# Edge stage of a graph attention layer: running sums kept in two accumulator banks, queries in two rounded parts, a product in four instructions

## What is computed

```python
qkv = (h @ W_qkv + b_qkv).reshape(n, 3, H, DH)        # H = 8 heads of DH = 32
q, k, v = (qkv[:, 0], qkv[:, 1], qkv[:, 2])
score = jnp.einsum('ehd,ehd->eh', q[dst], k[src]) * SCALE
mx = jax.ops.segment_max(score, dst, num_segments=n)
ex = jnp.exp(score - mx[dst])
denom = jax.ops.segment_sum(ex, dst, num_segments=n)
attn = ex / denom[dst]
msg = attn[:, :, None] * v[src]
h_new = jax.ops.segment_sum(msg, dst, num_segments=n)
h_out = jnp.transpose(h_new, (0, 2, 1)).reshape(n, DIM)
return (h_out + h) @ W_out + b_out
```

## Time and profile before

| what | value |
|---|---|
| three runs, us | 2121.98, 2125.84, 2130.7 (median 2125.84) |
| span of the profiled execution, us | 2134.3 |
| mean granted clock of TensorE | 0.903 |
| busy over the whole span | PE 83%, DVE 72%, POOL 54%, ACT 50% |
| gathers of the edge stage (L1740) | 440, busy 476.1 us, mean 1082 ns, idle before them 135.8 us |
| queries (L1822) | 880 matmul records, busy 233.7 us, mean 407 ns |
| sums (L1853) | 880 matmul records, busy 226.2 us, mean 402 ns |
| message product (L1896) | 110, mean 1219 ns |

### The profile page before, as it was taken

One profiled execution on the slowest core, in us unless ns is written; L12 is line 12 of the kernel. 1 busy time (PEld: TensorE's weight loads), 2 busy tenths in 40 slices (PEclk: granted clock), 3 DMA queues, 4 the chain that ended last, 5 costly groups with the idle time before them and its releaser, 6 DMA issues. The chain is left out here.

```text
span 2134.3 us, 41549 instructions
## 1 busy us (share of the span) xinstructions
PE 1761.5 (83%) x10388; PEld 1537.1 (72%) x10389; DVE 1539.6 (72%) x2788; ACT 1070.3 (50%) x2353; POOL 1160.5 (54%) x1169
## 2 busy tenths in 40 slices
PE   3699999999999989828973868888888888866278
PEld 3499999999999979728972756666666766645267
DVE  5388888888888845643545849899999898847622
ACT  1677777777777726403420145445455454316133
POOL 0376666666666601462443457777777777512112
PEclk7799999999999989758996989999999999867579
DMA  3443333333333312133323566666666666524310
GB/s 96 133 121 111 104 108 108 104 107 108 105 106 108 98 31 80 69 124 98 119 75 98 193 185 189 189 188 188 193 191 186 190 187 188 148 65 141 115 38 29
DMA packets 132538, 267.55 MB, mean 125 GB/s; under 512 B 24030, under 2 KB 75888, under 8 KB 132407
## 3 DMA queue, kind: packets, MB, share of 16 engines
q0 software_dynamic: 63456, 191.61, 30.7%
q1 hardware_dynamic: 68534, 73.21, 11.2%
q10 hardware_dynamic: 416, 1.18, 0.2%
HBM read 225.34 MB, written 42.50 MB: 125 GB/s over the span
## 5 line engine op out<-in xcount | busy, mean ns | idle before, releaser
L319 POOL DMA_INDIRECT e_rows<-h_table,e_idx x440 | 453.4, 1030 | 214.1 <-issue 106.3
L1740 POOL DMA_INDIRECT a_rows<-kv_table,a_idx x440 | 476.1, 1082 | 135.8 <-issue 128.9
L619 PE MATMUL e_w<-w2h,e_hidl 128*128 128x256 f32 x880 | 247.7, 304 | 2.9 <-DVE e_msg L704 2.9
L589 PE MATMUL e_agg<-e_msg,e_hot 128*128 128x256 f32 x880 | 246.1, 402 | 0.0
L1822 PE MATMUL a_q<-q,a_spread 128*128 x880 | 233.7, 407 | 6.5 <-ACT a_spread L1782 6.3
L620 PE MATMUL e_w<-w2l,e_hidh 128*128 128x256 f32 x880 | 226.4, 280 | 0.0
L1853 PE MATMUL a_agg<-a_rows,x 128*128 128x264 f32 x880 | 226.2, 402 | 0.0
L704 DVE TENSOR_TENSOR e_msg<-e_w,e_rows 128x1024 f32<-128x1024 f32 x110 | 134.7, 1224 | 93.4 <-PE e_w L623 93.4
L1775 ACT ACTIVATE a_apart<-iota_n,dst_rel 128x128 f32<-128x128 f32 x440 | 140.6, 391 | 112.9 <-PE a_agg L1853 112.8
L1822 PEld LDWEIGHTS a_q<-q,a_spread 128*128 128x128 f32 x880 | 166.2, 199 | 38.9 <-issue 12.8
L1853 PEld LDWEIGHTS a_agg<-a_rows,x 128*128 128x128 f32 x880 | 168.2, 200 | 24.7
(11 more groups left out here) (456 smaller groups left out, 4221.4 us busy)
## 6 DMA issues: line engine op xcount, KB each, us to landing
e_ea<-in_eaT SPq DMA_DIRECT2D x220, 64.0 KB
m_rows<-expert_rows SPq DMA_DIRECT2D x32, 272.0 KB, 2.7
e_rows<-h_table,e_idx POOLq DMA_INDIRECT x440
a_rows<-kv_table,a_idx POOLq DMA_INDIRECT x440, 3.7
q_ab<-expert_out SPq DMA_DIRECT2D x50, 128.0 KB, 3.3
kv_table<-q_kv SPq DMA_DIRECT2D x25, 256.0 KB, 2.2
u_stage<-in_m_w SPq DMA_DIRECT2D x16, 256.0 KB
x<-in_x SPq DMA_DIRECT2D x1, 3200.0 KB, 13.9
```

The source lines that it names most:

```text
L319: c.nc.gpsimd.indirect_dma_start(out=rows[:, g.slot8, j, :], out_offset=None, in_=table, in_offset=bass.IndirectOffsetOnAxis(ap=idx[:, g.s ...
L589: last = mm(bank(wins[j]), hot[:, g.slot4, t, :], msg[:, g.slot4, t, :], start=False, stop=False, skip_group_check=True)
L619: mm(w, hidl[:, g.slot, cols[k]], w2h[:, k, :], start=(k == 0), stop=False)
L1740: nc.gpsimd.indirect_dma_start(out=rows[:, g.slot * IG + j, 0:2 * D], out_offset=None, in_=c.kv_dram, in_offset=bass.IndirectOffsetOnAxis( ...
```

## The change

Attention stage, window sums: they stay in PSUM. There are two banks, chosen by the window's parity; PE adds each item to the bank of its window (`add_item`), ACT copies the bank to `c.sums` after every item (`keep`), and the other bank is cleared by the two-column first instruction of each `add_item`. The sums run one step later (SUM = 7). DVE's addition is gone; its rescale works on the PSUM bank, at place 3 instead of 2, from a copy of the factors that ACT makes (`grown`). The first item's sum goes between the second and third query, or behind the queries at place 3; the second stays behind the transposes. `hot` has 12 slots. `c.sums` and the query parts now share one space, shifted by a window: a copied-out sum lies where a query was that is no longer needed.

Queries: `c.q` in float32 becomes `c.qhl`, a rounded float32r part and the rounded rest; each tile's query is two float32r matmuls. ACT makes the first part in `project_qkv`, POOL the second, ten windows behind.

Message product: four instructions of one tile instead of one of four.

POOL's clearing of `c.sums` is gone; the PSUM banks are zeroed by four ACT copies at the start of the stage.

```diff
@@ -1418,10 +1418,12 @@
+        q = c.sb("q_q", [P, GT, D], F32, s)
+        s_qh, s_ql = c.sem("q_qhigh"), c.sem("q_qlow")
...
@@ -1453,13 +1455,24 @@
+                BEHIND = 10
+                def query_low(t):
+                    need(pool, s_pg, (s_qh, t + 1))
+                    high, low = c.qhl[:, t, 0:D], c.qhl[:, t, D:2 * D]
+                    nc.gpsimd.tensor_tensor(low, q[:, t % GT, :], high.bitcast(F32), ALU.subtract).then_inc(s_ql, 1)
                 for t in range(NW):
                     need(pool, s_pg, (s_ab[t % RING], (t // RING + 1) * 16 * TOPK))
                     nc.gpsimd.tensor_tensor(ab[:, t % RING, 0, :], ab[:, t % RING, 0, :], ab[:, t % RING, 1, :], ALU.add).then_inc(s_pr, 1)
                     need(pool, s_pg, (s_pr, t + 1))
                     nc.gpsimd.tensor_tensor(window(c.x, t), window(c.x, t), ab[:, t % RING, 0, :], ALU.add).then_inc(s_x, 1)
-                nc.gpsimd.memset(c.sums[:, :, :], 0.0).then_inc(s_clr, 1)
-                pool.wait_ge(s_clr, 1)
+                    if t >= BEHIND:
+                        query_low(t - BEHIND)
+                for t in range(NW - BEHIND, NW):
+                    query_low(t)
+                pool.wait_ge(s_ql, NW)
...
@@ -1490,6 +1503,12 @@
+                def query_high(t):
+                    need(act, s_ag, (s_s, t + 1))
+                    nc.scalar.copy(c.qhl[:, t, 0:D], q[:, t % GT, :]).then_inc(s_qh, 1)
...
@@ -1501,6 +1520,10 @@
                         need(act, s_ag, (s_t, t + 1), (s_r, t - GT + 1))
                         nc.scalar.copy(xTh[:, t % GT, :, :], by_chunk(tp[t % 2])).then_inc(s_hi, 1)
+                    t = r - 1
+                    if inside(t):
+                        query_high(t)
+                query_high(NW - 1)
             @block.vector
             def _(dve):
@@ -1529,8 +1552,8 @@
-                        need(dve, s_dg, (s_ld, 32), (s_r, t + 1), (s_kv[t % GT], (t // GT) * 16))
-                        v.tensor_tensor(window(c.q, t), qp[t % 2][:, 0:D], b[:, 0:D], ALU.add)
+                        need(dve, s_dg, (s_ld, 32), (s_r, t + 1), (s_kv[t % GT], (t // GT) * 16), (s_ql, t - GT + 1))
+                        v.tensor_tensor(q[:, t % GT, :], qp[t % 2][:, 0:D], b[:, 0:D], ALU.add)
...
@@ -1688,11 +1711,13 @@
     nc = c.nc
     R, DM, ROW, LAG = Edges.RING, D + H, 2 * D + H, 6
+    SUM = LAG + 1
+    HR = 12
...
-        spread = c.sb("a_spread", [P, 2, IG, P], F32, s)
+        spread = c.sb("a_spread", [P, 2, IG, P], F32R, s)
...
@@ -1705,11 +1730,14 @@
-        hot = c.x[:, :, :].rearrange("p t d -> p (t d)")[:, 0:R * IG * P].rearrange("p (s n) -> p s n", n=P)
+        hot = c.x[:, :, :].rearrange("p t d -> p (t d)")[:, 0:HR * IG * P].rearrange("p (s n) -> p s n", n=P)
...
-        ap = c.ps("a_agg", [P, JG, 512], F32, s)
-        none = c.sb("a_none", [P, DM], F32R, s)
-        s_none = c.sem("a_none")
+        ap = c.ps("a_agg", [P, 2, 512], F32, s)
+        zero = c.x[:, :, :].rearrange("p t d -> p (t d)")[:, HR * IG * P:NW * D]
+        none = c.sb("a_none", [P, P], F32R, s)
+        s_zero, s_none = c.sem("a_zeroed"), c.sem("a_none")
+        bank = lambda w: ap[:, bass.ds(w & 1, 1), 0:DM].rearrange("p a d -> p (a d)")
+        other = lambda w: ap[:, bass.ds((w + 1) & 1, 1), 0:DM].rearrange("p a d -> p (a d)")
...
@@ -1718,7 +1746,10 @@
+        grown = c.sb("a_grown", [P, H], F32, s)
+        s_gn = c.sem("a_grown")
         four = lambda g: slice(g.slot * IG, (g.slot + 1) * IG)
+        hots = lambda g, j: (g.n % HR) * IG + j
...
                 nc.gpsimd.memset(none[:, :].bitcast(F32), 0.0).then_inc(s_none, 1)
+                nc.gpsimd.memset(zero[:, :], 0.0).then_inc(s_zero, 1)
...
-                        need(pool, c.sem("poolgate"), (s_idx, g.n + 1), (s_agg, g.n - R + 1))
+                        need(pool, c.sem("poolgate"), (s_idx, g.n + 1), (s_agg, (g.n - R + 1) * JG))
...
@@ -1744,9 +1776,22 @@
+                act.wait_ge(s_zero, 1)
+                for p in range(2):
+                    nc.scalar.copy(ap[:, p, 0:D], zero[:, :])
+                    nc.scalar.copy(ap[:, p, D:DM], zero[:, 0:H]).then_inc(s_zero, 1)
+                def keep(a, j, wins):
+                    need(act, s_ag, (s_agg, a.n * JG + j + 1))
+                    nc.scalar.copy(window(c.sums, wins[j])[:, 0:DM], bank(wins[j])).then_inc(s_acc, 1)
                 def step(at):
                     i = at(0)
+                    a = at(-SUM)
+                    if real(a):
+                        wins = item_windows(act, c, a.n)
+                        keep(a, 0, wins)
...
@@ -1770,16 +1815,21 @@
-                        need(act, s_ag, (s_agg, g.n - R + 1), (s_hot, g.n))
+                        need(act, s_ag, (s_agg, (g.n - HR + 1) * JG), (s_hot, g.n))
...
-                        nc.scalar.activation(hot[:, four(g), :], apart[:, :, :], ACT.Relu, bias=1.0, scale=-1.0).then_inc(s_hot, 1)
+                        nc.scalar.activation(hot[:, hots(g, 0):hots(g, IG), :], apart[:, :, :], ACT.Relu, bias=1.0, scale=-1.0).then_inc(s_hot, 1)
...
+                    if i.place == 2 and closed(i.chunk - 1):
+                        need(act, s_ag, (s_gr, i.chunk), (s_rs, 2 * (i.chunk - 1)))
+                        nc.scalar.copy(grown[:, :], grow).then_inc(s_gn, 1)
+                    if real(a):
+                        keep(a, 1, wins)
...
@@ -1798,65 +1848,76 @@
+                def add_item(m, j, both):
+                    own = (both + j) >> 1
+                    need(pe, None, (s_msg, m.n + 1), (s_acc, m.n * JG + j), *([(s_rs, 2 * m.chunk + 2)] if m.place == 0 and j == 0 else []), own=True)
+                    mm(other(own)[:, 0:2], none[:, :], none[:, 0:2], start=True, stop=False, skip_group_check=True)
+                    for half in range(CT):
+                        t = j * CT + half
+                        last = mm(bank(own), hot[:, hots(m, t), :], rows[:, m.slot * IG + t, D:ROW], start=False, stop=False, skip_group_check=True)
+                    last.then_inc(s_agg, 1)
                 def step(at):
...
-                        need(pe, None, (s_sc, min(i.n, NIG) if isinstance(i.n, int) else i.n), (s_rs, 2 * ch), own=True)
+                        need(pe, None, (s_sc, min(i.n, NIG) if isinstance(i.n, int) else i.n), (s_gn, ch), own=True)
...
+                    m = at(-SUM)
+                    sums = ahead.take(i.step, "sums", m.n) if real(m) else None
+                    late = i.place == 3
                     g = at(1)
+                    if real(m) and not real(g):
+                        add_item(m, 0, sums)
                     if real(g):
                         both = ahead.take(i.step, "q", g.n)
                         wins = both >> 1, (both + 1) >> 1
                         need(pe, None, (s_sp, g.n + 1), (s_pr, g.n - 1), own=True)
                         for j in range(IG):
+                            if j == CT and real(m) and not late:
+                                add_item(m, 0, sums)
                             if j == CT and i.place == 2 and closed(ch):
...
-                            last = mm(qp[g.pair][:, j * D:(j + 1) * D], spread[:, g.pair, j, :], window(c.q, wins[j // CT]), start=True, stop=True)
+                            both_parts = window(c.qhl, wins[j // CT])
+                            mm(qp[g.pair][:, j * D:(j + 1) * D], spread[:, g.pair, j, :], both_parts[:, 0:D], start=True, stop=False)
+                            last = mm(qp[g.pair][:, j * D:(j + 1) * D], spread[:, g.pair, j, :], both_parts[:, D:2 * D], start=False, stop=True)
                         last.then_inc(s_q, 1)
+                        if real(m) and late:
+                            add_item(m, 0, sums)
...
-                    m = at(-LAG)
-                    if real(m):
-                        moved = ahead.take(i.step, "sums", m.n) & 1
...
-                    if real(at(1 - LAG)):
-                        ahead.fetch(i.then, "sums", at(1 - LAG).n)
+                    if real(at(1 - SUM)):
+                        ahead.fetch(i.then, "sums", at(1 - SUM).n)
                     h = at(2)
                     if real(h):
                         need(pe, None, (s_hot, h.n + 1), (s_sp, h.n), own=True)
                         for j in range(IG):
-                            last = tr(hT[:, j * P:(j + 1) * P], hot[:, h.slot * IG + j, :], c.ident[:, :])
+                            last = tr(hT[:, j * P:(j + 1) * P], hot[:, hots(h, j), :], c.ident[:, :])
                         last.then_inc(s_ht, 1)
                     if i.place == 2 and closed(ch):
                         need(pe, None, (s_fi, 2 * ch + 2), (s_ex, ch + 1), own=True)
                         mm(grow, first[:, :], diag[:, :], start=True, stop=True).then_inc(s_gr, 1)
                     if real(m):
-
-                        need(pe, None, (s_msg, m.n + 1), (s_acc, m.n), own=True)
```

(47 more changed lines are left out.)

5 lines of the change are left out of this document (2 added, 3 removed).

## The result

The changed kernel takes 2190.28 us (median, 2188.22 to 2195.08) against 2126.73 (2121.98 to 2130.70) for the kernel before: ratio 1.0302, 95% interval 1.0283 to 1.0321. It is slower by 63.5 us; 15.9 were forecast, with a range up to 2168.

A forecast was written before the change was run, and what follows sets the result against it. POOL's stream was taken to pace the edge stage, at 22.15 us a chunk. Chunks +6.8, drain +7.2, projection +1.0 and start +0.9 gave +15.9 us: 2150 on the profiled 2134.3, 2142 on the median 2125.84; range 2100 to 2168.

The forecast's parts named there:

- Place 2 to 3: Edge stage, the chunk's longer step, through copies, four products, reductions, rescale and item 0: 7.13 us.
- Item 0 and its start, 1.11 + 0.03: Term of the ACT-PE round: item 0's matmuls 1.11 us, its two-column start 0.03 more (estimate), together 1.14.
- Two queries, 0.48: Term of the ACT-PE round: two queries in two parts each, 4 × 0.12 = 0.48 us.
- Place 0 to 1, 5.09 as every plain step: Edge stage: round from one copy of item 0 to the next, 5.09 us, counted three times a chunk.
- Chunk 22.40: Edge stage: 3 × 5.09 + 7.13 = 22.40 us a chunk against 22.15, over 27 chunks +6.8 us.
- The drain, 49.9: Sums left after the queries end: 8 × 2 × 3.12 = 49.9 us against 42.7 before, +7.2 us.
- Projection and start, +1.9: POOL's 25 subtractions in the projection, +1 us, and ACT's four zeroing copies at the start, +0.9; POOL's clearing gone, 0.
- The clock did not fall: Rival, edge stage: the clock falls once a chunk, +22 us on the forecast, 2164 us; chance 0.15.
- The split does let gathers through: Rival, four products don't let gathers through: POOL needs 22.6 a chunk, +12 instead of +6.8, 2147; counted in the forecast.
- POOL as the bound: Rival, edge stage: POOL stays the bound, its stalls go, 20.4 us a chunk, −38, 2088 us; chance 0.21.
- The drain did not run at 2.4 GHz: Rival "no difference": chunk as computed, drain at 2.4 GHz, −5.9 us, in all +2.8, 2129 us; chance 0.20.
- the four products do overlap: Rival, place 2 to 3: four products don't overlap, 4 × 0.42, 0.32 more per chunk, +8.6, 2151 us; chance 0.06.

The follow-up runs named there:

- e5: The kernel before with float32r queries and spread, one matmul per tile without the rounded rest: 2133.23 us, ratio 1.0022.
- e4: The kernel before with the message product in four instructions and nothing else changed: 2137.60 us, ratio 1.0052.
- e2: The changed kernel with the message product in one instruction of 1024 elements again: 2179.60 us, ratio 1.0254.
- e1: The changed kernel with the two-column clearing behind an item's matmuls instead of ahead (except the last item before a rescale): 2158.77 us, ratio 1.0152.
- e7: The changed kernel with the carries' matmul at place 1 behind item 0 instead of ahead of the queries: 2180.00 us, ratio 1.0242.
- e8: The changed kernel with the clearing behind the item, one message product and the carries' matmul behind item 0 together: 2136.59 us, ratio 1.0042.
- e13: The kernel before with POOL's clearing of the sums in 26 pieces of one window instead of one at the end: 2122.16 us, ratio 0.9971.
- e3: The changed kernel with one ACT copy per group behind spread and both items added together at the end of PE's step: 2551.99 us, ratio 1.2009.
- e9: e8 with another ACT order: spread ahead of the Abs, copy of item 1 behind them, Relu last: 2139.44 us, ratio 1.0063.

## Why the prediction was wrong

**Right.** What bounded the kernel before (POOL's stream; e5 shows that PE did not). That the copies of ACT and the items of PE make a round, and its way, term by term. That fewer held gathers and shorter queries bring nothing by themselves (e4, e5; DVE's addition was not taken away alone). That the direction is slower. Place 2 to 3 was forecast at 7.13 and measured at 7.29, and the rule of the Trainium skill (VectorE: DVE Perf Modes, "The TRN2 errata — SBUF-src ops pay a fixed extra latency per instruction") against small instructions proved right in its direction: four products cost 0.24 us in the path (e2). The sum for four that overlap, 1.36, was still nearer than the 1.70 that its formula gives, for the four take 1.40 to 1.49 us, 1.42 in the median, from the first start to the last end:

```profile
1512.48 0.27 ACT L1806 COPY a_rows<-a_misc 128x128 f32<-128x128 f32 x1
1512.90 1.43 DVE L1961 TENSOR_TENSOR a_rows<-a_rows 128x256 f32<-128x256 f32 x4 [2.13 <-ACT a_rows L1806]
1514.25 1.22 DVE L1967 TENSOR_TENSOR a_rows<-a_q,a_rows 128x1024 f32<-128x1024 f32 x1
1515.61 1.22 DVE L1990 TENSOR_REDUCE a_sc<-a_rows 128x32 f32<-128x1024 f32 x1
1516.75 0.42 DVE L1950 SCALAR_TENSOR_TENSOR a_agg<-a_grown,a_agg 128x256 f32 x1
...
1517.70 0.27 PE L1855 MATMUL a_agg<-a_none 128*128 128x2 f32 x1 [0.69 <-DVE a_agg L1952]
```

**The steps that failed.** The mechanism was forecast, its length was not: a chunk takes 23.91 us instead of 22.40. All but the last of these are terms of the sum that were too small:
- *Item 0 and its start, 1.11 + 0.03.* Measured 0.22 + 1.15 = 1.37. This is the largest of them: four times a chunk, and worth 31 us with its part in the drain (e1). The 0.03 was right where it could be read before. In the first layer the same kind of instruction, two columns on a bank chosen by registers, opens each item, and the item of the earlier trace rows starts 0.03 us behind it (405.54; the median of 220 is 0.03):

```profile
405.51 0.17 PE L586 MATMUL e_agg<-w2h,e_none 128*128 128x2 f32 x1
```

  There the register work for the item's address (one operation of 32 ns, one of 46) was done while earlier matmuls still streamed: it lies at 405.17 to 405.31. In the edge stage PE has just waited for `spread`, its queue has no lead, and the same two operations lie between the weight loads of the clearing (1510.47) and of the item (1510.68). In 219 of the 220 items the second operation lies between the two loads. In the first layer it does so in 7 of 220, and four of these seven have 0.20 to 0.23 us as well. So it is the address work behind a wait that takes the time, and not the two columns. That is read from the traces; no run takes the register work away and leaves the instruction, since the windows are known only to registers. The work for the clearing's own bank (ns min, median, max):

```profile
L1855 PEldq FUSED_REGOPS  x440: 46/58/77, 1275.8 to 1947.5; - x147
L1855 PEldq ALU_OP  x220: 32/32/36, 1275.9 to 1947.4; - x110
```

- *Two queries, 0.48.* Measured 0.58 in the median, 0.63 in the step shown. The matmuls are 0.12 apart as forecast, but for the second of the four, which starts 0.22 behind the first in the median of all groups. The first is the one behind the wait for `spread`: its weight load starts only 7 ns before it, and it lasts 0.38 instead of 0.28. The register operation for the second's address is not the reason: it lies between the two weight loads in 84 of 110 groups and not in the other 26, and the distance is 0.22 in both. The sum had such an exposed load only in place 2 to 3.
- *Place 0 to 1, 5.09 as every plain step.* The carries' matmul ahead of the queries was left out of the sum: 0.40 us a chunk, 10.3 us in all (e7).
- *Chunk 22.40* was 23.91: 0.32 more in each of the three plain steps (the item 0.23 and the queries 0.10; the other terms were right within 0.02 each), 0.16 from place 2 to 3, which had 0.20 for an exposed load, and 0.40 for the carries. 1.51 × 27 = 41 us; with the 6.8 forecast that makes 47.6. From the first gather to the end of the last query the profiles show 46.5 (654.7 us against 608.2); the stream of gathers shows 41.0 of it, since the last gather now stands 4.8 us ahead of the end of the last query and stood 0.7 behind it. In e8, where the clearing and the carries are out of the path, the plain step is 5.15 against the forecast 5.09.
- *The drain, 49.9*, was 62.4 at clock 0.55, and the 42.7 that it was compared with left out the first 5.4 us behind the last query: alike it was 48.1, so the drain grew by 14.3 and not by 7.2. A plain item took 3.56 instead of 3.12 (3.61 from copy end to copy end in these rows):

```profile
1909.31 0.38 ACT L1787 COPY sums<-a_agg  x1 [3.74 <-PE a_agg L1858]
1910.20 0.37 PE L1855 MATMUL a_agg<-a_none 128*128 128x2 f32 x1 [1.25 <-ACT sums L1787]
1910.43 2.11 PE L1858 MATMUL a_agg<-a_rows,x 128*128 128x264 f32 x4
1912.92 0.38 ACT L1787 COPY sums<-a_agg  x1 [3.23 <-PE a_agg L1858]
```

  The way back from ACT to PE is 0.51 (end 1909.69 to 1910.20), register work included, not 0.20, which was taken from the handoff to the first query; the item is 0.23 + 2.11, not 2.16. The 62.4 us hold seventeen items and not sixteen: the first, of the group whose step had the last query, is copied out after 2.8 us and was not in the sum. The other sixteen take 59.5, where 16 × 3.56 = 57.0. The first of these still runs at clock 1.00 (2.9 us), and some of the others are up to 0.9 longer than a plain one: carries, exponentials and rescales of the last chunks stand in the same queues, and the sum left them out.
- *Projection and start, +1.9*: the first gather comes 88.1 us after the first addition instead of 93.4, −5.3, though POOL has 25 instructions more. That the clearing goes was put at 0 because "nobody waited long" behind it; that looked for waits at semaphores only, and not for an instruction that runs twelve times as long beside it (5.11 us instead of 0.41, under e13).

**Rivals.** The clock did not fall (0.99 in the window, 0.98 before). The split does let gathers through. POOL as the bound did not come either: it idles 1.00 us (median) in front of each group's first gather, 0.30 in the kernel before. The range failed on its upper side because every bound in it was a bound of a single term; that several small terms of one round are too short at once was not among the cases, and the round is run in each of 110 steps. The drain did not run at 2.4 GHz (clock 0.55), and the four products do overlap (1.42 us, not 1.68).

## What to carry to other kernels

Before handing a stage's work to an idle engine, write out the round that the handover closes, instruction by instruction in the order of both queues, and count every step of it, the register work and the small opening instruction too: here the 0.22 us between the start of an opening instruction on two columns and that of the next matmul cost 31 us, and a row from a place where the queue runs ahead of its engine had shown 0.03. Then look at what stands in front of each link in its queue; two of the experiments gained 15 and 31 us by moving nothing but an order. And look for the next-longest round before taking one away: e3 and e9 each only exchanged it. When the difference of two drains goes into a sum, let both begin at the same event.
